# Two-layer mixer kernel: the expert stage written out without a loop, weights resident, token chunks outermost, router operations between the experts' products

## The reference, cut to what matters

```
t = to_tokens(x)                       # 2048 tokens of 64 channels
flat = layernorm(t)
logits = flat @ router_w.T             # 8 experts
probs = softmax(logits)
p, idx = top_k(probs, 2); p = p / (sum(p) + 1e-9)
gates = p spread over the 8 experts, zero for the other six
h1 = einsum('nc,ehc->neh', flat, w1); h3 = einsum('nc,ehc->neh', flat, w3)    # 682 hidden per expert
y = einsum('neh,ech->nec', silu(h1) * h3, w2)
x = from_tokens(t + einsum('ne,nec->nc', gates, y))
```

## Time and profile before

| what | us |
|---|---|
| median of the three runs | 956.11 |
| the three runs | 960.1, 953.72, 956.11 |
| profiled execution, from its first to its last instruction | 952.8 |

### The profile page before, as it was taken

How to read it: one execution, slowest core, us unless ns; L and a number is a source line. 1 busy time by engine, 2 the same in 40 slices (tenths; PEclk the granted TensorE clock), 3 DMA queues, 4 the chain that set the end, 5 groups by cost and what they waited for, 6 DMA issues and landing times.

```text
span 952.8 us, 18695 instructions
## 1 busy us (share of the span) xinstructions
PE 800.3 (84%) x6356; PEld 594.2 (62%) x6356; DVE 570.5 (60%) x1752; ACT 556.2 (58%) x1664; POOL 366.6 (38%) x297
## 2 busy tenths in 40 slices
PE   5899987777777776789988768999689999899995
PEld 3587875555655555566666547889446666466663
DVE  3888854556456466334344346887457667467765
ACT  3676752333355365334444355777478888588884
POOL 0878620000000000003000007874268888588884
PEclk7999995555555555555555556999689999899998
DMA  9700000000001100000000000000000100200001
GB/s 224 175 2 1 2 1 1 1 1 1 0 1 78 78 1 1 1 0 1 1 1 1 1 1 1 2 1 2 1 1 2 59 21 2 80 1 2 2 1 23
DMA packets 5860, 18.54 MB, mean 19 GB/s; under 512 B 1093, under 2 KB 2822, under 8 KB 5254
## 3 DMA queue, kind: packets, MB, share of 16 engines
q1 hardware_dynamic: 5478, 17.21, 6.2%
q10 hardware_dynamic: 288, 0.13, 0.1%
HBM read 9.47 MB, written 0.52 MB: 10 GB/s over the span
## 4 chain that ended last, share of the span: by engine, by line
PE 41%; POOL 22%; DVE 13%; issue 11%; ACT 11%; DVEq 1%; POOLq 1%; DMA 0%; SPq 0%; ACTq 0%
POOL zw L1007 21%; PE bank L558 10%; PE bank L383 6%; PE bank L560 6%; PE bank L400 6%; DVE bank L1320 5%; PE bank L348 4%; DVE hr L1324 4%; ACT bank L885 4%; ACT bank L889 4%; PE bank L524 2%; PE bank L370 1%; DVE hid L1089 1%; PE bank L315 1%; PE bank L413 1%
## 5 line engine op out<-in xcount | busy, mean ns | idle before, releaser
L1007 POOL TENSOR_TENSOR zw<-hid,zw 128x512 f16<-128x512 f32 x176 | 203.9, 1159 | 49.3 <-ACT zw L928 38.9
L558 PE MATMUL bank<-hr,lv 64*64 64x8 f32 x512 | 97.0, 261 | 98.8 <-DVE hr L1324 98.4
L966 POOL TENSOR_TENSOR st<-tent,tentx 128x768 f32<-128x768 f32 x72 | 112.2, 1589 | 173.3 <-DVE tentx L1081 123.8
L1443 DVE SCALAR_TENSOR_TENSOR hid<-bank,wsc,st 128x512 f32<-128x512 f32 x176 | 131.9, 750 | 76.0 <-ACT st L932 70.1
L558 PEld LDWEIGHTS bank<-hr,lv 64*64 64x64 f32 x512 | 72.8, 201 | 158.4 <-DVE hr L1324 158.2
L885 ACT ACTIVATE bank<-bank 64x16 f32<-64x16 f32 x256 | 39.2, 153 | 196.8 <-PE bank L560 196.5
L604 PE MATMUL bank<-st,wh 128*128 128x512 f16 x352 | 136.9, 389 | 11.5 <-POOL st L1000 5.4
L932 ACT ACTIVATE st<-bank,wsc 128x512 f32<-128x512 f32 x176 | 120.9, 687 | 39.8 <-PE bank L605 22.0
L605 PE MATMUL bank<-st,wl 128*128 128x512 f16 x352 | 136.8, 389 | 0.0
L966 POOL TENSOR_TENSOR st<-sq 128x768 f32<-128x768 f32 x9 | 13.2, 1498 | 309.3 <-DVE sq L1309 308.5
L1320 DVE TENSOR_TENSOR_SCAN bank<-bank,scan_add 64x24 f32<-64x24 f32 x256 | 52.9, 207 | 127.8 <-ACT bank L885 127.5
(11 more groups left out here) (184 smaller groups left out, 1340.4 us busy)
## 6 DMA issues: line engine op xcount, KB each, us to landing
w13s<-w SPq DMA_DIRECT2D x8, 704.0 KB, 17.9
w2f<-w SPq DMA_DIRECT2D x4, 384.0 KB, 25.4
w13s<-wh SPq DMA_DIRECT2D x2, 704.0 KB, 3.7
w13s<-wl SPq DMA_DIRECT2D x2, 704.0 KB, 5.0
wh<-w13s SPq DMA_DIRECT2D x2, 704.0 KB, 3.9
wl<-w13s SPq DMA_DIRECT2D x2, 704.0 KB, 5.1
w2f<-w2p SPq DMA_DIRECT2D x2, 384.0 KB, 4.9
w2p<-w2f SPq DMA_DIRECT2D x2, 384.0 KB, 5.7
```

The costliest lines, as they stand in the source:

```text
L558: nc.tensor.matmul(both[:, 0, t, :], lv[:, C:2 * C], prev, start=False, stop=True, skip_group_check=True)
L966: nc.gpsimd.tensor_tensor(st[p][:, t, k:k + KG, :].rearrange("p k (y x) -> p k y x", x=16), ty, tx, ALU.mult)\
L1007: nc.gpsimd.tensor_tensor(hl[:, u % MR, :], hid[:, u % MR, :], hh[:, u % MR, :], ALU.subtract)\
L1443: nc.vector.scalar_tensor_tensor(out=hid[:, u % MR, :], in0=bank[2 + u % 2][:, :], scalar=wsc[:, 5:6], in1=silu[:, u % 2, :], op0=ALU.mult ...
```

## The change

- **No loop, other order.** All 176 units are written out. Chunks are the outer order (`CHUNKS = (0, 2, 1, 3)`), pairs the inner. There are four sets of weight tiles, all filled before the stage, so nothing is stored back or fetched during it. The two gate copies go; `gather` reads its gates where they were made.
- **Weights prepared in two halves.** The untouched weights have room for two pairs only. Pairs 0 and 1 are loaded and their maxima taken (n = 4 to 31), pairs 2 and 3 loaded over them (maxima n = 44 to 71), these split (high parts from n = 88), pairs 0 and 1 loaded again and split (from n = 128). Counts of operations stay as they were.
- **Tokens by chunk.** ACT makes high parts and scaled tokens in six operations of 512 columns instead of three of 1024, POOL the low parts in four instead of two; PE waits for chunk one only.
- **Router spread.** After the first exponential, the router's 21 operations on DVE go in eleven pieces of mostly two behind the `hid` of units 0 to 10.
- **Half the result midway.** When the first two chunks are through all pairs, `summed(0)` goes behind `hid` 95, four transposes behind `second(96)`, `result(0)` behind `hid` 99, and SP stores two of the four DMAs. PE's `second` of the group after waits for that result, since it shares bank 6. The other half stays at the end.

The diff, cut to its core:

```diff
+UNITS = PAIRS * NCH * PT
+CHUNKS = (0, 2, 1, 3)
+GROUPS = PAIRS * NCH
@@ sync: loads
+            def load_pair(e, signal):
+                for hf in range(2):
+                    sp.dma_start(w13s[hf * C:hf * C + C, e % 2, :], w13[e]).then_inc(s(signal), 16)
+                sp.dma_start(w2f[:, e % 2, :, :], w2[e]).then_inc(s(signal), 16)
...
+            for e in range(2):
+                load_pair(e, "ld_w0")
+            sp.wait_ge(s("w_part"), 2 * PAIRK)
+            for e in range(2, 4):
+                load_pair(e, "ld_w1")
+            for e in range(2):
+                sp.wait_ge(s("w_split"), e + 1)
+                load_pair(e, "ld_w2")
@@ tensor
-            pe.wait_ge(s("m_parts"), 2)
-            U = 2 * NCH * PT
-            with pe.Fori(0, PAIRS // 2) as i:
+            pe.wait_ge(s("w_split"), PAIRS)
+            def first(u):
+                g, k0 = u // PT, u % PT * 128
+                e, tok = g % PAIRS, CHUNKS[g // PAIRS] * CH
+                if u % (PAIRS * PT) == 0:
+                    pe.wait_ge(s("m_parts"), g // PAIRS + 1)
+                pe.wait_ge(s("m_hid"), u + 1)
...
+            def second(u):
+                g, t = u // PT, u % PT
+                if t == 0:
+                    pe.wait_ge(s("m_acc"), 2 * g + 2)
+                    if g == GROUPS // 2 + 1:
+                        pe.wait_ge(s("m_out"), 1)
...
+            def turn_result(q):
+                pe.wait_ge(s("m_sum"), q + 1)
+                for j in range(JJ):
+                    mm = nc.tensor.transpose(bank[6][:, j * 128:j * 128 + 128],
+                                             sq[:, q * 512 + j * 128:q * 512 + j * 128 + 128], ident[:, :])
+                mm.then_inc(s("m_tr"), 1)
+            for u in range(UNITS + MLAG):
+                if u < UNITS:
+                    first(u)
+                if u >= MLAG:
+                    second(u - MLAG)
+                if u == (GROUPS // 2 + 1) * PT:
+                    turn_result(0)
+            turn_result(1)
@@ scalar
+            for q in range(2):
+                act.wait_ge(s("n3_xn"), q + 1)
+                high_tokens(q)
+                scaled_tokens(q)
+                high_tokens(2 + q)
@@ vector
+            def route(n):
+                if n == 0:
+                    note(nc.vector.reduce_sum(red[1], col(0), AX.X))
+                    note(nc.vector.reciprocal(red[2], red[1]))
+                elif n == 1:
+                    note(nc.vector.tensor_tensor(col(2), col(0), wide(red[2]), ALU.mult))
+                    note(nc.vector.reduce_max(red[3], col(2), AX.X))
+                elif n == 2:
+                    note(nc.vector.tensor_tensor(col(3), col(2), wide(red[3]), ALU.is_equal))
+                    note(nc.vector.tensor_tensor(col(4), col(3), rank, ALU.mult))
...
+            halfway = GROUPS // 2 * PT
+            for u in range(UNITS):
+                dve.wait_ge(s("m_silu"), u + 1)
+                dve.wait_ge(s("m_h"), 2 * u + 2)
+                nc.vector.scalar_tensor_tensor(out=hid[:, u % MR, :], in0=bank[2 + u % 2][:, :],
+                                               scalar=wsc[:, 5:6], in1=silu[:, u % 2, :],
+                                               op0=ALU.mult, op1=ALU.mult).then_inc(s("m_hid"), 1)
+                if u < 11:
+                    route(u)
+                if u == PT:
+                    dve.wait_ge(s("m_zero"), 1)
+                if MLAG <= u % PT < MLAG + 4 and u > PT:
+                    gather(u // PT - 1, u % PT - MLAG)
+                if u == halfway + MLAG + 4:
+                    summed(0)
+                elif u == halfway + PT:
+                    result(0)
```

More of the change, by code:

```diff
@@ L590, in _ @@
             mm.then_inc(s("m_log"), 1)
-            pe.wait_ge(s("m_parts"), 2)
-            U = 2 * NCH * PT
-            with pe.Fori(0, PAIRS // 2) as i:
[L594 to L624, removed]
-                for u in range(U + MLAG):
-                    if u < U:
-                        first(u)
-                    if u >= MLAG:
-                        second(u - MLAG)
@@ L923, in _, with high @@
             nc.scalar.preload_act_table(ACT.Silu)
[L924 to L936 removed]
+            def high(u):
+                act.wait_ge(s("m_hid"), u + 3)
+                nc.scalar.copy(hh[:, u % MR, :], hid[:, u % MR, :]).then_inc(s("m_hh"), 1)
+            for u in range(UNITS):
+                act.wait_ge(s("m_h"), 2 * u + 1)
+                nc.scalar.activation(silu[:, u % 2, :], bank[u % 2][:, :], ACT.Silu, scale=wsc[:, 4:5])\
+                    .then_inc(s("m_silu"), 1)
+                if u > 0:
+                    high(u - 1)
+            high(UNITS - 1)
         @block.gpsimd
@@ new lines, in gather @@
+            def gather(g, n):
+                k, ch = n // 2, CHUNKS[g // PAIRS]
+                e = 2 * (g % PAIRS) + k
+                dve.wait_ge(s("m_y"), g + 1)
+                dve.wait_ge(s("m_acc"), 2 * g + k + 4)
+                for jj in range(n % 2 * 2, n % 2 * 2 + 2):
+                    j, hf = ch % 2 * JJ + jj, ch // 2
+                    mm = nc.vector.scalar_tensor_tensor(
+                        out=acc[:, j, hf, :],
+                        in0=bank[4 + 2 * (g % 2) + jj // 2][:, (2 * (jj % 2) + k) * 128:][:, 0:128],
+                        scalar=g1[:, j, hf, e:e + 1], in1=acc[:, j, hf, :],
+                        op0=ALU.mult, op1=ALU.add)
+                if n % 2 == 1:
+                    mm.then_inc(s("m_acc"), 1)
@@ L1451, in _, with summed @@
             parts = acc.rearrange("p j h (k c) -> p (j h) k c", k=2)
-            for q in range(2):
+            def summed(q):
+                dve.wait_ge(s("m_acc"), 4 + GROUPS * (q + 1))
                 half = slice(8 * q, 8 * q + 8)
@@ L1455, in _, with result @@
                                         parts[:, half, 0, :], parts[:, half, 1, :], ALU.add).then_inc(s("m_sum"), 1)
-            for q in range(2):
+            def result(q):
                 dve.wait_ge(s("m_tr"), q + 1)
                 nc.vector.tensor_tensor(xs[:, q * 512:q * 512 + 512], xs[:, q * 512:q * 512 + 512],
-                                        bank[6 + q][:, :], ALU.add).then_inc(s("m_out"), 1)
+                                        bank[6][:, :], ALU.add).then_inc(s("m_out"), 1)
+            halfway = GROUPS // 2 * PT
+            for u in range(UNITS):
+                dve.wait_ge(s("m_silu"), u + 1)
[13 more added lines that the diff above has]
+                    result(0)
+            for n in range(4):
+                gather(GROUPS - 1, n)
+            summed(1)
+            result(1)
 def kernel(**inputs):
```

263 lines of the change are left out of this document (106 added, 157 removed).

## The result

| | before | after |
|---|---|---|
| median, us | 955.06 (4 runs, 953.72 to 960.1) | 940.43 (4 runs, 937.08 to 943.09) |
| span of the profiled execution | 952.8 | 935.3 |

The ratio is 0.984, interval 0.981 to 0.987: 14.6 us faster. The profiled execution of after took 937.08 by the device, 1.8 above its span. It is the fastest of its four runs, so the two spans differ by more, 17.5, than the medians. A reader should take the terms from stretches inside the profiles, not from the two spans.

The account below looks back on a forecast made before the run. PE was taken to bound the steady stage at 14.84 us a group. The terms, -8.1 - 4.8 + 1.5 - 1.3 = -12.7 with 0 for the recurrence, took 956.1 to 943.4, range 938.5 to 952.

Parts of the forecast that it names:

- What bounds the kernel: Steady stage: PE is the bound, 14.84 us a group of eleven units, and no part of the change alters this.
- Term 1: Turn of the loop between the passes: stop for instructions, drain, refill and half clock go, -8.1 us.
- Rival E: At the turn something as long as the stop remains, gain there only 3.0: 948.5; chance 0.12 together with Rival C.
- Term 2: Start of the stage: earlier first `hid`, router spread over units 0 to 10 at 1.7 us a unit, -4.8 us.
- Rival A: Units 0 to 10: every router piece loses a full POOL subtraction, P = 2.6, 9.0 worse: 952.4; chance 0.12.
- Rival B: Router's units: PE stays at half clock, 2.6 us a unit: 952.4; chance 0.06.
- Term 3: Midway half result: four transposes on PE and a sum on DVE that waits for POOL, +1.5 us.
- Rival C: Midway: the handover empties the pipeline as the turn did, 5.1 comes back: 948.5; chance 0.12 together with Rival E.
- Term 4: End of the kernel: two of four DMA issues go, -1.3 us.
- Term 5: Recurrence: same counts of operations, the weight load in the middle hides with 1.7 us to spare, 0.
- Rival D: Recurrence: the weight reload comes late and stops step 44 for 15.5 us: 958.9; chance 0.05.
- The launch part: Outside the span: the median lies 3.3 us above the span and nothing at launch changes.

Follow-up runs that it names:

- b_no_drain: The kernel before with one stream of 176 units in old order, no loop or drain between passes, weights still stored and fetched: 947.24, ratio 0.991.
- a_result_at_end: The kernel after with both halves of the result summed, turned, added and stored at the end, none midway: 938.49, ratio 0.982.
- a_again: The kernel after, unchanged, with a second profile and more runs: 940.59, ratio 0.983.
- b_written_out: The kernel before with its two passes written out without the loop; drain between passes and weight fetches stay: 951.88, ratio 0.996.
- a_router_ahead: The kernel after with all eleven router pieces ahead of the first `hid` instead of between the first eleven: 944.01, ratio 0.987.

## Why the prediction was right, point by point

The forecast was 943.4, range 938.5 to 952; measured 940.43. The four terms gave -12.7, the same stretches give -14.8. Of the 3.0 between forecast and median, 2.1 is the terms; the other 0.9 is scatter of the medians (before's went from 956.11 to 955.06 with its fourth run). The measured time lies close to the range's good end, which took three terms at their best; added up again from the terms, that best is 940.0 and not 939.8.

- **What bounds the kernel**: right. PE's 14.84 a group is unchanged (units 110 to 175 take 87.5 in both).
- **Term 1, the turn, -8.1**: right to the hundredth (8.11 by `b_no_drain`), and so was the choice of 8.1 over 3.0. Rival E is refuted: PE of after has no idle time at unit 88, and the branch alone was 3.65.
- **Term 2, the start, -4.8: the step that was mis-sized; it is -6.05 (5.98 at unit 10, where it was forecast).** The first `hid` comes 7.67 earlier against 8.0 forecast, held by the table load as said. The period P of units 0 to 10 was put at 1.7 and is 1.56, which accounts for 1.4 over ten distances; unit 10's subtraction stands 1.5 behind its `hid`, not 1.6. Two parts of it failed. The floor of 1.43 summed recorded durations, though the record of `hid` overlaps the next start by 0.08; without the lock the units are 1.29 apart. And not every piece waited for a subtraction. Then `hid` 11 to 13 came 1.26, 0.96 and 1.25 apart, less than the steady 1.31, but of this 0.46 only 0.07 reached POOL's subtractions by unit 16. Given how the start scatters, the miss is 0.7 to 2.4.
- **Rival A, the lock at its strictest, P = 2.6**: refuted, though the lock is in most pieces. A piece that is held makes the next `hid` late, and this moves the next subtraction too, as argued. Longest distance: 1.98.
- **Rival B, half clock through the router's units**: refuted. The granted clock in after is back at 1.00 at 688.8, 7.7 after the first product; in before it was 698.7, 9.4 after it.
- **Term 3, midway, +1.5: over-sized; it is +0.86** (by after and by `a_result_at_end`). The sum on DVE did wait for POOL and took 1.60, just the 0.9 + 0.69 forecast. But PE showed 0.41 of it, not 0.8, and the transposes cost 0.44, not 0.6: again a record that overlaps the next. The result cost nothing. Rival C is refuted.
- **Term 4, the end, -1.3**: measured -1.5 against before's profile. Against the kernel with both halves at the end it is 0.8 to 1.3, by the kernels that end as after does.
- **Term 5, the recurrence, 0**: right, with the landing at 215.10 for 215.3. It had 1.1 us to spare until the scan of that step and 2.0 until DVE's first read of it; 1.7 was forecast. Rival D was possible and did not happen.
- **The launch part**: 956.11 stood 3.3 above the span of an execution that was not the median one. In each profile here whose own time is given, time less span is 1.8. The other 1.5 was scatter, and harmless, since the sum was set against the median.

The profiled execution of after came out at 935.3, 4.8 under the 940 that was to show the forecast right. Of this, 2.1 is the terms and 2.7 chance ahead of the stage, as `a_again`'s 939.6 bears out. One profiled span on its own is no test of a forecast here.

## What to carry to other kernels

Price the turn of a loop by the distance between the same unit of one pass and of the next, less the steady units between: the stall that a row names was 3.04 of 8.1 here, and the rest went only when the pipeline was carried across the turn. Small work pushed into the gaps of an engine costs the distance to the next start, not its recorded duration, and on DVE, if it has two inputs in SBUF (here even one tensor and a column of scalars), it also waits for POOL's subtraction; give it an input in PSUM, or a place where POOL is idle. When a change has several parts, run each alone: here resident weights and the half result midway brought nothing that the measurement shows, and the gain came from the one written-out stream, the spread router and the earlier start that chunks allow (1.7 of its size as far as the runs part it).

## What the runs showed beyond that

The second convolution has no part in the change, yet it took 108.9 us in some profiles and 110.3 to 111.4 in others, from the last scan to the first matmul of `norm(3)`, with the same work. The windows right behind the last scan of after, of `a_again` and of before (the column ahead of the last two is the granted clock):

```profile
559.30:573.30 14.00, 9.72 (x50) 6.84 (x50) 6.20 (x16) 9.73 (x25) 1.23 (x1) 0.64 0.00 0
```

```profile
562.80:576.80 14.00, 10.54 (x45) 7.14 (x44) 5.81 (x15) 9.03 (x22) 1.26 (x1) 0.50 0.00 0
```

```profile
559.70:573.70 14.00, 10.54 (x45) 7.19 (x45) 5.85 (x15) 9.06 (x22) 1.22 (x1) 0.50 0.00 0
```

PE is at half clock through the recurrence. Where the clock rose 10 to 11 us after the last scan (in six of the twelve profiles, after's first one and `b_written_out`'s among them), the stretch took 108.9; where it rose some 14 us after or later, 110.3 to 111.4. Before had its lasting rise 26 after and took longest. Two profiles of the same code stand on either side, so it is no trait of a kernel. That the clock's rise is the cause is read from these twelve profiles; no run changed it alone. This is up to 2.5 us, a good part of the scatter between runs. The next stretch scatters the same way: from the first matmul of `norm(3)` to `xn` it is 9.4 to 9.6 in the four profiles whose clock fell to half within 0.4 us of that matmul (before, after, `a_again`, `a_router_ahead`), and 7.2 to 8.1 in the eight whose clock fell 4 to 7 us behind it. The first scan's own place, 145.9 to 150.9 over the profiles, scatters as much, and why was not tried.
